# Layer normalisation moved from VectorE to ScalarE in a two-layer attention, Mamba and expert kernel

## The chip, the cores and the metric

The kernel runs on one core of one Trainium2 chip. The metric is the device time of one execution in microseconds (us); three runs are given by their median. The engines are TensorE (PE in the profile, its weight loads PEld), VectorE (DVE), ScalarE (ACT), GpSimd (POOL) and SyncE (SP), which only issues transfers here.

## The reference

```python
x = L0_attn_x                      # [8, 512, 128]: 8 batches of 512 tokens, float32
xn = _layernorm(x)                 # (x - mean) / sqrt(var + 1e-5), over the 128 features
s = attention(xn)                  # q, k, v; no token attends to itself; softmax
g = _silu(experts(xn))             # 8 experts of 256, two per token, gated
x = x + s * g
xn = _layernorm(x)
s = mamba(xn)                      # rmsnorm, in_proj, conv of 4 taps, selective scan
                                   # (256 channels x 16 states), out_proj, + xn
g = _silu(switch_experts(xn))      # 8 experts of 512, one per token, with a norm of its own
x = x + s * g
```

## The kernel before

The 8 batches are handled one after the other; 512 tokens lie as 4 tiles of 128 tokens (one token per partition, 128 features along the row), and after a transpose as one tile of 128 features by 512 tokens. All arithmetic of the matrix products is float32.

The work of a batch is cut into groups of steps: A is the first layer (layer norm `ln0` and `xn`, transpose `xT`, gate logits `gl` and `gate`, `q`, `k`, `v`, scores `s`, transposes `p` of the weights, output `o`, expert products `h` and `m`, and `silu`, which adds the result to x and signals `x1`). H is the head of the second layer (`ln1`, `xm`, transposes `hT` and `x1T`, `xi` and `z` with the convolution, `u`, `bc`, `dl`, `ln`, `du`, and the routing `sc`, `rk`, `put`). S is the scan: 32 steps, each with a decay `d` on ACT, a product with B and a scan on DVE (lines 1296 and 1303), a product with C on POOL (`p`, line 1470), and sums over states on PE (`a`, line 888) or POOL (`e`, line 1477); `b` spreads a row of B over the partitions on PE (line 877), `c` loads a row of C. F is the second expert layer on tokens sorted by expert (`xs`, `h`, `y`, `get`, `ft`, `silu`), and C the end of a batch (`y`, `op`, `out`).

Every engine works through one list that is written before the kernel starts. A table `ROWS` gives for each step its place in an iteration, counted in iterations of 32 scan slots, then offsets in slots for ACT, DVE and POOL, and the PSUM bank that it uses. Group A runs two batches ahead of the scan, H one ahead, C one behind, so one iteration holds A of batch b+2, H of b+1, S and F of b and C of b-1. A second table, `OWN`, has places of their own for A and H of batch 0 and A of batch 1, which make up the prologue. An engine is strictly in order: a step that waits holds up all that stands behind it on its engine. PE and SP follow the places alone.

The two layer norms are made in three parts. DVE takes mean and variance of each token (`moments`, lines 1118 and 1121). POOL computes `rstd` = (var + eps) to the power -0.5, and for the second norm also `rstd2`, the scale of the rmsnorm that follows it. DVE then writes `(x - mean) * rstd` tile by tile, as `xn` (line 1146) into `xn_tok` and as `xm` (line 1214) into `xn1_tok`. In the step `xm` ACT scales `xn1_tok` by `rstd2` into `ht_tok` (line 1001), from which PE makes `hT`. In the trace `qkv` stands for the tensor that holds `xn_tok`, `xn_tok` for the one written by `xm`, and `hx` for `ht_tok` and `hT`. Almost all of ACT's work is recorded under line 944.

## Time and profile before

| | |
|---|---|
| median of 3 runs | 982.8 us (982.41 to 982.96) |
| the profiled execution | 983.75 us |
| its span, first to last instruction | 981.9 us |
| PE busy | 855.8 us, 87% |
| DVE busy | 810.0 us, 82% |
| ACT busy | 608.9 us, 62% |
| POOL busy | 587.6 us, 60% |
| mean granted TensorE clock | 0.936 of full speed |

The profile is of one execution. Busy time is the time in which an engine runs an instruction; the chain that ended last is followed backwards from the last instruction, at each step to what released it or to what stood before it on its engine. A group of instructions is named by line, engine, operation and tiles (output <- inputs), and the idle time in front of it by what ended it.

### The profile page before, as it was taken

To read this page: it belongs to the slowest core of one execution; us is meant where nothing else is said; L and a number is where in the kernel's file an instruction comes from. 1 tells how busy PE (TensorE), PEld (TensorE's weight loads), DVE (VectorE), ACT (ScalarE), POOL (GpSimd) and SP (SyncE) were. 2 spreads that over 40 slices of the span, in tenths; PEclk is the share of its full clock that TensorE was granted. 3 is DMA by queue.
4 is the path that set the end of the run, shared out by engine and by line. 5 is a ranking of instruction groups with operands and counts; after the bars stand their busy time and mean duration, and the time that the engine had idled before them with its cause. 6 is when DMAs were issued, how large, how long until landed. Compare 5 with 4: busy or idle time off the path is not lost.

```text
span 981.9 us, 15767 instructions
## 1 busy us (share of the span) xinstructions
PE 855.8 (87%) x4624; PEld 582.9 (59%) x4624; DVE 810.0 (82%) x1542; ACT 608.9 (62%) x1315; POOL 587.6 (60%) x524
## 2 busy tenths in 40 slices
PE   5997897999699978999799969999799977684995
PEld 3773475766467745766477736776477645452762
DVE  4244537999989889999999998998999989886995
ACT  3424644868467766778477765778477765574661
POOL 0010202848856695848766694848765697669665
PEclk9977699999899999999999998999999989796998
DMA  7200103224323334324323243225322234324542
GB/s 263 88 0 1 44 12 105 72 80 97 115 65 90 96 94 128 76 76 121 94 89 93 75 115 99 76 78 131 100 85 79 77 101 138 98 72 113 156 132 51
DMA packets 79428, 90.27 MB, mean 92 GB/s; under 512 B 8450, under 2 KB 49906, under 8 KB 78834
## 3 DMA queue, kind: packets, MB, share of 16 engines
q1 hardware_dynamic: 77298, 85.07, 29.5%
q0 software_dynamic: 2048, 4.20, 1.5%
q8 instruction: 40, 0.66, 0.3%
q14 instruction: 42, 0.34, 0.1%
HBM read 52.96 MB, written 13.04 MB: 67 GB/s over the span
## 4 chain that ended last, share of the span: by engine, by line
PE 55%; DVE 21%; issue 9%; POOL 8%; ACT 5%; SPq 1%; DMA 1%; DVEq 0%; POOLq 0%
PE work L823 10%; PE work L829 9%; DVE st L1303 7%; PE work L854 5%; PE yacc L888 5%; PE work L864 5%; PE work L752 3%; POOL st L1470 3%; PE work L773 3%; DVE b_row L1296 2%; PE work L796 2%; PE work L743 2%; PE b_row L877 2%; ACT prob L944 1%; PE work L725 1%
## 5 line engine op out<-in xcount | busy, mean ns | idle before, releaser
L1470 POOL TENSOR_TENSOR st<-st,Cs 128x512 f32<-128x512 f32 x249 | 316.8, 1278 | 178.1 <-DVE st L1303 162.9
L944 ACT ACTIVATE dA<-delta,Aneg 128x512 f32<-128x512 f32 x256 | 175.5, 723 | 20.6 <-POOL du L1431 10.7
L888 PE MATMUL yacc<-st,w_ident 128*128 128x512 f32 x256 | 143.6, 650 | 19.5 <-POOL st L1470 19.1
L1303 DVE TENSOR_TENSOR_SCAN st<-dA,dbu 128x512 f32<-128x512 f32 x128 | 154.7, 1209 | 1.4 <-PE yacc L888 0.6
L1303 DVE TENSOR_TENSOR_SCAN st<-dA,b_row 128x512 f32<-128x512 f32 x123 | 148.7, 1209 | 3.1 <-POOL y L1477 3.1
L829 PEld LDWEIGHTS work<-w_w2a,hid 128*128 128x128 f32 x1024 | 124.3, 195 | 29.4 <-issue 13.0
L944 ACT ACTIVATE hsT<-work,hs 128x128 f32<-128x128 f32 x352 | 99.7, 370 | 61.0 <-PE work L854 60.3
L823 PE MATMUL work<-xnT,w_w1a 128*128 128x512 f32 x256 | 134.5, 615 | 0.7 <-ACT dt L944 0.7
L1477 POOL TENSOR_TENSOR y<-y,st 128x512 f32<-128x512 f32 x105 | 133.2, 1269 | 3.0
L829 PE MATMUL work<-w_w2a,hid 128*128 128x128 f32 x1024 | 127.3, 279 | 5.2 <-ACT hid L944 5.2
L944 ACT ACTIVATE hid<-work,w_b1a 128x512 f32<-128x512 f32 x128 | 87.9, 688 | 66.5 <-PE work L823 62.1
L1188 DVE SCALAR_TENSOR_TENSOR acc<-work,gates,acc 128x128 f32<-128x128 f32 x256 | 71.0, 339 | 50.0 <-PE work L829 46.2
L854 PEld LDWEIGHTS work<-xsT,hs 128*128 128x128 f32 x704 | 92.6, 202 | 20.8 <-issue 12.3
L854 PE MATMUL work<-xsT,hs 128*128 128x128 f32 x704 | 98.2, 287 | 1.2 <-ACT hsT L944 1.2
L864 PE MATMUL work<-w_w2f,hsT 128*128 x704 | 98.8, 284 | 0.0
L864 PEld LDWEIGHTS work<-w_w2f,hsT 128*128 128x128 f32 x704 | 86.4, 193 | 20.0 <-issue 17.8
L1296 DVE TENSOR_TENSOR dbu<-b_row,du 128x512 f32<-128x512 f32 x123 | 85.4, 695 | 14.8 <-PE b_row L877 7.3
L1296 DVE TENSOR_TENSOR b_row<-b_row,du 128x512 f32<-128x512 f32 x123 | 84.0, 683 | 2.7
L877 PE MATMUL b_row<-bc,sel_b 96*128 96x512 bf16 x123 | 48.8, 400 | 35.5 <-DVE st L1303 35.5
L888 PEld LDWEIGHTS yacc<-st,w_ident 128*128 128x128 f32 x256 | 46.0, 204 | 56.3 <-POOL st L1470 28.6
L1418 POOL TENSOR_TENSOR ve<-mv,eps 128x4 f32<-128x4 f32 x16 | 3.2, 201 | 113.9 <-DVE mv L1121 113.9
L1440 POOL DMA_INDIRECT xs_dram<-xn_tok,pos x32 | 32.5, 1016 | 51.9 <-DVE pos L1271 43.7
(187 smaller groups left out, 1315.0 us busy)
## 6 DMA issues: line engine op xcount, KB each, us to landing
Cs<-c_dram SPq DMA_DIRECT2D x128, 256.0 KB
hs<-w_w1f SPq DMA_DIRECT2D x88, 258.0 KB, 2.4
xs_in<-xs_dram SPq DMA_DIRECT2D x16, 256.0 KB
ys_dram<-ys SPq DMA_DIRECT2D x16, 256.0 KB, 2.2
w_w1f<-in_w1f_dram SPq DMA_DIRECT2D x1, 2064.0 KB, 7.7
x_in<-in_x_dram SPq DMA_DIRECT2D x8, 256.0 KB
w_w2f<-in_w2f_dram SPq DMA_DIRECT2D x1, 2048.0 KB, 12.8
kept_dram<-x_tok SPq DMA_DIRECT2D x8, 256.0 KB, 2.4
```

The costliest lines, as they stand in the source:

```text
L823: last = mm(w[:], W["w1a"][:, i * 128:(i + 1) * 128], xnT[:], start=True, stop=True)
L829: last = mm(w[:, t * 128:(t + 1) * 128], hid[:, c % 4, t * 128:(t + 1) * 128], W["w2a"][:, c * 128:(c + 1) * 128], start=(c == PER * i), s ...
L854: last = mm(w[:, c * 128:(c + 1) * 128], w1s[:, i % 2, c * 128:(c + 1) * 128], xsT[:, i // 4 % 2, i % 4 * 128:(i % 4 + 1) * 128], start=Tr ...
L864: last = mm(r, hsT[:, i % 2, c * 128:(c + 1) * 128], W["w2f"][:, bass.ds(e * H1 + c * 128, 128)], start=False, stop=(c == HC - 1))
L877: mm(rows_bank(n, b)[:], row_of(n), bc3[:, par], start=True, stop=True).then_inc(sig["B_in"], 1)
L888: mm(yacc[:], ident[:], state(s), start=False, stop=(n == NS - 1)).then_inc(sig["y_sum0"], 1)
L944: return nc.scalar.activation(out, in_, func, **k)
L1188: last = V.scalar_tensor_tensor(acc[:, t], w[:, t * 128:(t + 1) * 128], gates[:, t, i:i + 1], acc[:, t], ALU.mult, ALU.add)
L1296: V.tensor_tensor((dbu0, rows_bank(n, b))[h][:], rows_bank(n, b)[:], du[:, par, h], ALU.mult).then_inc(sig["dBu"], 1)
L1303: V.tensor_tensor_scan(state(s), dA[:, s % DECAYS], (dbu0, rows_bank(n, b))[h][:], 0.0, ALU.mult, ALU.add).then_inc(sig["scan"], 1)
L1470: G.tensor_tensor(state(s), state(s), Cs[:, b.of(NS, n) % C_BUFS], ALU.mult).then_inc(sig["P"], 1)
L1477: G.tensor_tensor(y1[:], y1[:], state(s), ALU.add).then_inc(sig["y_sum1"], 1)
```

## The change

The last part of both norms moves from DVE to ACT. ACT computes `x * rstd + shift` per token, as one activation with a scale and a shift per partition, and POOL makes `shift` = 0 - mean * rstd by two more operations on 128x4 elements, linked to the one before by waits. ACT's step `xn` is new in its list; its step `xm` now makes `xn1_tok` first and then, as before, `ht_tok`. Two waits come with it: ACT's `xm` waits for `opx` of two batches before, the last reader of the half of `xn1_tok` that it overwrites; DVE's write of `x_tok` waits for `xn1` of the batch before. All places, offsets and prologue places are new. The order of the groups and their distance in batches stay. The lines of `ROWS` that the prediction speaks of:

```diff
...
-    ("F", "xs", 0, 0.01820, 1, 5, 7, 0),
...
-    ("A", "xT", 0, 0.05523, 0, 2, 0, 1),
...
-    ("A", "ln0", 0, 0.03157, -1, -1, -1, None),
-    ("A", "xn", 0, 0.06785, 0, -2, -2, None),
...
-    ("A", "gl", 0, 0.08355, 1, 1, 6, 0),
...
-    ("A", "q", 0, 0.09246, 1, 7, -1, 3),
...
-    ("A", "k", 0, 0.08641, -1, 7, 2, 2),
...
-    ("H", "ln1", 0, 0.30272, -3, -2, -1, None),
-    ("H", "xm", 0, 0.24559, 5, 3, -4, None),
...
-    ("H", "cw", 0, 0.69621, -4, 1, 3, None),
...
-    ("A", "m", 6, 0.88321, 8, 0, 4, 1),
...
-    ("S", "c", 15, 0.87337, -1, 6, 3, None),
-    ("A", "m", 7, 0.91105, 8, 1, 3, 3),
...
-    ("H", "keep", 0, 0.86292, -1, 7, -3, None),
-    ("H", "fetch", 0, 0.99456, 3, 7, 2, None),
...
+    ("F", "xs", 0, 0.00177, 1, 7, 1, 3),
...
+    ("A", "xT", 0, 0.06669, -1, -1, 3, 3),
...
+    ("A", "ln0", 0, 0.03416, -1, -1, -1, None),
+    ("A", "xn", 0, 0.04999, 0, -1, -4, None),
...
+    ("A", "gl", 0, 0.07446, -1, 0, 8, 0),
...
+    ("A", "q", 0, 0.12685, -2, 7, -3, 3),
...
+    ("A", "k", 0, 0.10789, -1, 7, 0, 3),
...
+    ("H", "ln1", 0, 0.28984, -4, -3, -4, None),
+    ("H", "xm", 0, 0.29673, 1, 3, -4, None),
...
+    ("H", "cw", 0, 0.99045, -2, 4, 0, None),
...
+    ("A", "m", 6, 0.95524, 7, 0, 1, 1),
...
+    ("S", "c", 15, 1.00111, 4, 7, 2, None),
+    ("A", "m", 7, 0.96005, 5, 1, 5, 2),
...
+    ("H", "keep", 0, 0.57657, 1, 7, -3, None),
+    ("H", "fetch", 0, 0.78823, 0, 7, 2, None),
...
```

The code:

```diff
@@ -494,6 +494,8 @@
         rstd1 = sb("rstd1", [128, NT])
         q2 = sb("q2", [128, NT])
         rstd2 = sb("rstd2", [128, NT])
+        shift, shift1 = sb("shift", [128, NT]), sb("shift1", [128, NT])
+        zeros = sb("zeros", [128, NT])
         xn1_tok = sb("xn1_tok", [128, 2, NT, D])
         xn1T = sb("xn1T", [128, T])
         u = sb("u", [128, 2, NH, T])
@@ -995,7 +997,17 @@
                 elif name == "hT":
                     filled(act, g, step, b)
                     go(hT, w[:], ACT.Copy).then_inc(fr, 1)
+                elif name == "xn":
+                    act.wait_ge(sig["rstd0"], b.of(1, 1))
+                    for t in range(NT):
+                        last = go(xn_tok[:, t], x_in[:, par, t], ACT.Identity, scale=rstd[:, t:t + 1], bias=shift[:, t:t + 1])
+                    last.then_inc(sig["xn0"], 1)
                 elif name == "xm":
+                    act.wait_ge(sig["rstd1"], b.of(1, 1))
+                    since(act, sig["opx"], b.of(1, -1))
+                    for t in range(NT):
+                        last = go(xn1_tok[:, par, t], x_tok[:, t], ACT.Identity, scale=rstd1[:, t:t + 1], bias=shift1[:, t:t + 1])
+                    last.then_inc(sig["xn1"], 1)
                     act.wait_ge(sig["xn1"], b.of(1, 1))
                     for t in range(NT):
                         last = go(ht_tok[:, t], xn1_tok[:, par, t], ACT.Copy, scale=rstd2[:, t:t + 1])
@@ -1140,12 +1152,6 @@
                 if name == "ln0":
                     dve.wait_ge(sig["x_in%d" % par], 16 * (b.n // 2 + 1))
                     moments(g, x_in[:, par], stats, mv, "mean0")
-                elif name == "xn":
-                    dve.wait_ge(sig["rstd0"], b.of(1, 1))
-                    for t in range(NT):
-                        last = V.tensor_scalar(xn_tok[:, t], x_in[:, par, t], mv[:, t, 0:1], rstd[:, t:t + 1],
-                                               ALU.subtract, ALU.mult)
-                    last.then_inc(sig["xn0"], 1)
                 elif name == "v":
                     filled(dve, g, step, b)
                     V.tensor_tensor(v_tok, tiles(w[:]), W["bv"][:].unsqueeze(1).broadcast_to([128, NT, D]), ALU.add
@@ -1202,18 +1208,13 @@
                     emptied(dve, g, ("o", NT - 1), b)
                     lk(g, V.tensor_tensor(r, r, s_tok, ALU.mult))
                     since(dve, sig["kept"], b.of(16))
+                    since(dve, sig["xn1"], b.of(1))
                     V.tensor_tensor(x_tok[:], x_in[:, par], r, ALU.add).then_inc(sig["x1"], 1)
                     dve.wait_ge(sig["x1"], b.of(1, 1))
                     dve.sem_inc(free_of(g, ("m", E - 1), b), 1)
                 elif name == "ln1":
                     dve.wait_ge(sig["x1"], b.of(1, 1))
                     moments(g, x_tok, stats1, mv1, "mean1")
-                elif name == "xm":
-                    dve.wait_ge(sig["rstd1"], b.of(1, 1))
-                    for t in range(NT):
-                        last = V.tensor_scalar(xn1_tok[:, par, t], x_tok[:, t], mv1[:, t, 0:1], rstd1[:, t:t + 1],
-                                               ALU.subtract, ALU.mult)
-                    last.then_inc(sig["xn1"], 1)
                 elif name == "xi":
                     dve.wait_ge(sig["cv_a"], b.of(NH, i + 1))
                     cw = W["conv_w"]
@@ -1395,6 +1396,7 @@
 
             V.memset(neghalf[:], -0.5)
             V.memset(eps[:], EPS)
+            V.memset(zeros[:], 0.0)
             V.memset(fe[:], 0.0)
             V.memset(ones_b[:], 1.0)
             V.memset(ones8[:], 1.0)
@@ -1416,7 +1418,9 @@
                     mv_k, ve_k, rstd_k = (mv, ve, rstd) if k == "0" else (mv1, ve1, rstd1)
                     pool.wait_ge(sig["mean" + k], b.of(1, 1))
                     lk(g, G.tensor_tensor(ve_k[:], mv_k[:, :, 1], eps[:], ALU.add))
-                    last = G.tensor_tensor(rstd_k[:], ve_k[:], neghalf[:], ALU.pow)
+                    lk(g, G.tensor_tensor(rstd_k[:], ve_k[:], neghalf[:], ALU.pow))
+                    lk(g, G.tensor_tensor(ve_k[:], mv_k[:, :, 0], rstd_k[:], ALU.mult))
+                    last = G.tensor_tensor((shift if k == "0" else shift1)[:], zeros[:], ve_k[:], ALU.subtract)
                     if name == "ln0":
                         last.then_inc(sig["rstd0"], 1)
                     else:
```

## Rows read from the trace of the kernel before

**Rows 1.** The page: busy time of each engine, and the chain that ended last.

```profile
PE 855.8 (87%) x4624; PEld 582.9 (59%) x4624; DVE 810.0 (82%) x1542; ACT 608.9 (62%) x1315; POOL 587.6 (60%) x524
...
PE 55%; DVE 21%; issue 9%; POOL 8%; ACT 5%; SPq 1%; DMA 1%; DVEq 0%; POOLq 0%
```

**Rows 2.** Windows: busy us of each engine in each stretch.

```profile
core 0: us, PE busy (x) PEld busy (x) DVE busy (x) ACT busy (x) POOL busy (x), PEclk, DMA share, GB/s
...
382.37:491.08 108.71, 100.01 (x569) 69.24 (x568) 100.14 (x190) 75.46 (x165) 75.93 (x68) 0.97 0.33 95
...
394.00:460.00 66.00, 65.76 (x402) 47.30 (x401) 61.62 (x112) 50.07 (x113) 46.53 (x43) 1.00 0.29 81
460.00:491.00 31.00, 22.55 (x96) 13.95 (x96) 28.13 (x51) 17.49 (x34) 25.34 (x23) 0.89 0.43 118
```

**Rows 3.** The chain that ended last, by line, of 460 to 491 us.

```profile
by line: DVE st L1303 22.1%; issue 15.3%; DVE acc L1188 6.7%; PE work L725 5.9%; DVE b_row L1296 4.8%; DVE qkv L1146 4.6%; DVE work L1276 4.6%; DVE work L1275 4.2%; DVE dbu L1296 4.2%; ACT L944 4.1%; DVE stats L1118 2.8%; PE work L722 2.6%;
```

**Rows 4.** Waits of 460 to 491 us: us in total, times, longest.

```profile
PE b_row L877 <- DVE st L1303: 4.9, 3, 2.4
...
PE work L847 <- ACT xsT L944: 1.6, 1, 1.6
...
PE yacc L886 <- DVE du L1317: 1.0, 1, 1.0
...
PE work L829 <- ACT hid L944: 0.9, 1, 0.9
```

**Rows 5.** Groups of the two normalisations on DVE, whole run.

```profile
L1214 DVE TENSOR_SCALAR xn_tok<-x_tok,mv,rstd 128x128 f32<-128x128 f32 x32 | 29.8, 992 | 3.3 <-POOL rstd L1428 3.3
...
L1146 DVE TENSOR_SCALAR qkv<-x_in,mv,rstd 128x128 f32<-128x128 f32 x32 | 11.4, 417 | 4.3 <-POOL rstd L1419 4.3
```

**Rows 6.** Timeline: `xm` on DVE beside POOL, and in the prologue.

```profile
406.10 4.12 DVE L1214 TENSOR_SCALAR xn_tok<-x_tok,mv,rstd 128x128 f32<-128x128 f32 x4
...
406.26 2.53 POOL L1470 TENSOR_TENSOR st<-st,Cs 128x512 f32<-128x512 f32 x2
...
66.17 1.11 DVE L1214 TENSOR_SCALAR xn_tok<-x_tok,mv,rstd 128x128 f32<-128x128 f32 x4 [3.33 <-POOL rstd L1428]
```

**Rows 7.** ACT's activations by group; a run of four; two pieces of the chain.

```profile
L944 ACT ACTIVATE hid<-work,w_b1a 128x512 f32<-128x512 f32 x128 | 87.9, 688 | 66.5 <-PE work L823 62.1 <-issue 2.1 <-PE work L829 2.0
...
L944 ACT ACTIVATE cv<-work,w_conv_b,w_conv_w 128x512 f32<-128x512 f32 x16 | 12.6, 788 | 7.7 <-PE work L773 7.7
...
410.26 1.28 ACT L944 ACTIVATE hx<-xn_tok,rstd 128x128 f32<-128x128 f32 x4 [0.61 <-DVE xn_tok L1214]
...
406.27 1.79 PE work L829 x16
...
414.08 1.79 PE work L829 x16
```

**Rows 8.** Timeline: POOL's small linked operations.

```profile
401.86 0.20 POOL L1425 TENSOR_TENSOR q<-rstd 128x4 f32<-128x4 f32 x1
...
402.14 0.20 POOL L1426 TENSOR_TENSOR q<-q,mv 128x4 f32<-128x4 f32 x1
```

**Rows 9.** Timeline: around `xn` in the followed iteration.

```profile
483.11 2.17 ACT L944 ACTIVATE hsT<-work,hs 128x128 f32<-128x128 f32 x8 [0.30 <-PE work L854]
483.15 1.05 POOL L1419 TENSOR_TENSOR rstd<-ve,neghalf 128x4 f32<-128x4 f32 x1
...
484.88 1.42 DVE L1146 TENSOR_SCALAR qkv<-x_in,mv,rstd 128x128 f32<-128x128 f32 x4
...
487.47 0.60 ACT L944 ACTIVATE xnT<-work 128x512 f32<-128x512 f32 x1 [2.20 <-PE work L718]
```

**Rows 10.** Timeline: the first boundary, and the last layer norm.

```profile
157.26 2.06 DVE L1146 TENSOR_SCALAR qkv<-x_in,mv,rstd 128x128 f32<-128x128 f32 x4 [1.44 <-POOL rstd L1419]
...
830.20 1.01 POOL L1428 TENSOR_TENSOR rstd<-q,neghalf 128x4 f32<-128x4 f32 x1
...
837.86 1.09 PE L765 MATMUL work<-w_ident,hx 128*128 128x128 f32 x4 [3.51 <-ACT hx L944]
```

More of the change, by code:

```diff
@@ L325 @@
     ("A", 0): (
[4 rows of a table removed]
[4 rows of a table added]
     ),
     ("H", 0): (
-        -1.11900, -1.08467, -1.01476, -0.83547, -0.90068, -0.85797, -0.89443, -0.84069, -0.83471, -0.83140, -0.82978, -0.62226,
-        -0.81859, -0.79895, -0.81765, -0.90515, -0.81371, -0.74442, -0.61163, -0.90703, -0.69090, -0.71827, -0.58703, -0.54773,
-        -0.50916, -0.42023, -1.08490, -1.30874,
+        -1.11411, -1.06978, -1.05742, -0.89565, -0.90279, -0.83828, -0.88733, -0.81603, -0.81528, -0.80089, -0.79422, -0.57863,
+        -0.79157, -0.74780, -0.77419, -0.79303, -0.73709, -0.72833, -0.62595, -0.89555, -0.69538, -0.77574, -0.66455, -0.53536,
+        -0.45046, -0.49154, -0.77058, -0.61446,
     ),
     ("A", 1): (
[4 rows of a table removed]
[4 rows of a table added]
     ),
```

510 rows, old and new, of tables (OWN, ROWS) are left out of this document.

## The prediction, made before the changed kernel was run

> **What bounds the kernel now.** I read the page's head and chain first [rows 1]. The reader is to see that PE and DVE are busy 87% and 82% of the span, ACT and POOL 62% and 60%, and that the chain of work that ended last runs over PE for 55% and over DVE for 21%, over ACT for 5%. So two engines share the end between them, and work taken off DVE can count, but not all of it.
>
> Next the windows, by stage [rows 2]. From 164 to 819 us the kernel repeats one pattern: six iterations, of which one is 382.37 to 491.08, 108.7 us long. In it PE is busy 100.0 us, DVE 100.1, ACT 75.5, POOL 75.9. Cut in two, PE is full from 394 to 460 (65.76 of 66 us) and has holes from 460 to 491 (22.55 of 31 us, at a mean granted clock of 0.89), while DVE is busy 28.13 of these 31. The chain in the second part says it again [rows 3]: DVE's scan alone is 22.1%, and the DVE normalisation L1146 4.6%, that is 1.42 us. The waits in it [rows 4] name what PE lacks there: 4.9 us in which `b_row` waits for a scan, 1.0 us for L1317.
>
> So the iteration is PE's for some 66 us and mostly DVE's for some 31 us. But DVE is 93% busy in the first part too (61.62 of 66): it carries its backlog into the second.
>
> **The change, part by part.** *Off DVE.* Per batch four `xm` and four `xn` instructions. All 64 are 29.8 + 11.4 = 41.2 us of DVE's 810, 992 ns for one of `xm` (L1214) and 417 for one of `xn` (L1146) [rows 5]. In the iteration that I follow the four take 4.12 us, while POOL runs two 128x512 products back to back in 2.53 us; at 66 us, where POOL has nothing of that kind, four take 1.11 us [rows 6]. So the price on DVE is 4.12 us for `xm` and 1.42 us for `xn` [rows 6, 9]: 5.5 us of DVE's 100.1 per iteration. The Trainium skill's page "SBUF — State Buffer", section "Who interferes with whom", says why: some VectorE instructions and GpSimd's share a port pair, and the one that comes second waits out the whole instruction of the other, while ScalarE waits on neither. By it four `xm` would cost up to four POOL products, 5.1 us; the trace is near that with 4.12. With 5.1 the term of `xm` in the sum below would be 1.8 instead of 1.5.
>
> *Onto ACT.* Four activations with one per-partition operand take 1.28 us in a run; an operand more costs 0.10 us on 512 columns (788 against 688 ns) [rows 7]. Four with scale and shift are then 1.4 to 1.7 us; I take 1.6, since the added 0.1 can fall in each of the four. ACT gets 3.2 us more per iteration: 75.5 becomes 78.7 of 108.7. For `xm` the row scaling (`ht`) follows in the same step, so 1.6 + 1.3 = 2.9 us stand in front of what is next on ACT: the evacuation of `h3` and two decays. Expert product `m1`, the first to need `h3`, starts 8 us after `m0` (406.1 and 414.1 [rows 7]), and the decays run up to four ahead of the scans, so I cost this at nothing; if that cover is gone, it is 1.6 us per iteration. `xn` stands between the evacuations of F's `h0` and `h1`, where ACT now is idle 2.2 us, waiting for `xT` [rows 9].
>
> *Onto POOL.* Two linked operations on 128x4 more per layer norm, 0.20 us and 0.07 to 0.08 us of gap each, as the rows of `q2` show [rows 8]: 0.54 us per norm, 1.1 us per iteration, on the way from the moments to the signal. POOL is 75.9 of 108.7 us busy. The memset of `zeros` stands among its like at the start, while PE waits for the weights: nothing.
>
> *Waits added.* ACT waits for `opx` of two batches before (`xm`), and DVE's x1 for `xn1` of the batch before; both are one iteration old when they are asked, so they cost nothing. DVE no longer waits for `rstd0` and `rstd1`, with its scans queued behind.
>
> *Places.* PE's order at the boundary becomes `xT`, `y0`, `gl`, `op`, `k`, `q` (before: `xT`, `gl`, `k`, `q`, `op`), `m6` and `m7` come some two scan slots later, and F's first transpose gets bank 3 where the second has bank 0, so that the second no longer waits for ACT to empty the first (1.6 us of PE per iteration [rows 4]). PE then still waits 1.0 us for L1317, so I count this at nothing (bounds 0 and 1.6). On SP's queue `keep`, `cw`, `c15` and `fetch` move. The first three wait for signals older than their places. `fetch` now waits for the four `put` transfers ahead of `c13` and `c14`; POOL issues the puts in one run before state product `p21`, and `c13` serves `p26`, so this is nothing too, unless the puts are late, when POOL's products would wait. Nothing else in the tables removes work. The new order as such I put at nothing; what it can move is PE's idle time, 8.7 us of an iteration, and a third of that either way would be 3 us per iteration, 17 in all, which the cases A and C span.
>
> **The sum.** In the second part of the iteration `xn` leaves DVE [rows 9]: 1.42 off, 0.54 of POOL on, 0.9 us gained. For PE nothing is gained by it: `rstd0` comes at 484.2 + 0.5 = 484.7, `xn` ends at 486.3 as it does now, the evacuation of `h1` behind it at 487.4, and that of `xT` starts then, now at 487.5. The bounds for this term are 0 and 1.42. `xm` leaves DVE where PE is full, so it pays only through backlog: between 0 and 4.12 us. Half of it is 2.1, DVE's share of the chain (21%) times it 0.9; I take the middle, 1.5. Together 2.4 us per iteration, times six 14.4.
>
> Outside of the pattern [rows 10]: the first boundary (157 us) has DVE idle 1.44 us for `rstd0` and then 2.06 us in `xn`, 3.5 in all, of which DVE's scans can win up to 3.0; half, 1.5. In the last layer norm PE waits 3.51 us for `ht`, until 837.9; new, `rstd1` comes at 831.2 + 0.5, and 1.6 + 1.3 us on ACT with some 0.2 of hand-over end near 834.8: up to 3.0, of which I take 2.0, since scans bound the tail too. In the prologue the way to `hT` is one chain [rows 6]: 1.11 us becomes 1.6, and 0.54 comes on POOL's side, for which DVE waits 3.33 us there already: 1.0 us lost. The other prologue places only reorder what PE does when full, or when the Mamba chain is alone: nothing, within 3 us.
>
> Sum: 14.4 + 1.5 + 2.0 - 1.0 = 16.9 us. The profiled execution has 983.75 us, its span 981.9 and 1.85 around it; it becomes 966.9. The median of the runs is 0.95 us below the profiled time, so the prediction is 966 us.
>
> **The rivals.**
> *A, the whole release counts.* DVE is the bound all along: its 100.1 busy us and 8.6 us of hand-over per iteration move together. For it: 28.13 of 31 us busy in the second part. Against it: PE has no hole for 66 us [rows 2]. 5.0 us per iteration (5.5 less 0.54) are 30, with 5 outside (both upper bounds less the prologue's 1.0) 35: 948 us. Chance 0.14.
> *B, only a little counts.* PE binds, `xm` gives back nothing, `xn` 0.9 us: 5.4 + 2.5 outside, 975 us. For it: `xm` lies where PE is full. Against it: what PE lacks later is scans, and `xm` delays these. The Trainium skill's page "ScalarE: Activation LUTs", "Rules for kernel authors", wants additions and products on VectorE since it is the faster; by it the exchange is a loss of speed, which holds here for undisturbed instructions (1.11 against 1.28 us), not for `xm` as it runs. Chance 0.22.
> *C, ACT takes the place of DVE.* The 2.9 us block of `xm` and the 1.6 of `xn` delay `hid`, decays and `xnT` in ACT's queue. PE already waits for `hid` 0.9 us per iteration. If DVE's release is worth the 0.9 of B and all 3.2 us come on the chain, an iteration is 2.3 us longer: 14, with 1 lost outside 998 us; from half of the 3.2 it costs 0.7 each, 988 us. It decides if more than 0.9 us (B) to 2.4 us (mine) of the 3.2 lie on the chain. Against it: ACT is idle 33 us of each iteration. Chance 0.13.
> *D, nothing to be measured*: gains and the new order cancel, 983 us. Chance 0.06.
>
> **How the numbers follow.** Mine, 958 to 972 us, has 0.45. Faster is mine, A and B: 0.81. Same 0.06 (0.2%, 2 us, is about what a measurement of this kernel can tell), slower 0.13. For 8 in 10 the range runs from 954 (half of A left out) to 984 us (B and D whole, C left out).
>
> **What would show it.** DVE busy 41 us less (769), ACT 22 to 26 more (some 633), POOL 8 to 10 more plus nothing for its products. An iteration of 106.3 us. DVE's share of the chain below 21%, PE's above 55%. `b_row` waiting for scans less than 4.9 us per iteration. The normalisations on ACT near 480 ns each. Wrong: ACT above 10% of the chain, `hid` waits grown beyond 1 us per iteration (C), an iteration at 108 (B) or 104 (A), or DVE's scan inputs slower than 0.69 us because they now meet POOL more often.

## The result, and the profile after

The changed kernel takes 978.09 us in the median of 20 runs (974.61 to 984.63), the kernel before beside it on the same chip 981.47 us (20 runs, 979.82 to 983.40): a ratio of 0.9967, 95% interval 0.9951 to 0.9983, or 3.4 us faster. Forecast were 16.9. The changed kernel's runs spread over 10 us, those of before over 3.6. The profiled execution has 977.57 us and a span of 975.8, 6.1 below the span of before; against the medians' 3.4 some 2.7 us of these 6.1 are the choice of executions.

The page's head and chain, to be laid beside [rows 1]:

```profile
PE 854.6 (88%) x4624; PEld 583.0 (60%) x4624; DVE 777.3 (80%) x1479; ACT 632.0 (65%) x1379; POOL 592.7 (61%) x556
...
PE 53%; POOL 17%; DVE 15%; issue 10%; ACT 4%; SPq 1%; DMA 0%; DVEq 0%; POOLq 0%
```

The work went where it should: DVE is 32.7 us less busy, ACT 23.1 more, POOL 5.1 more. What the reader is to see is in the chain: DVE fell from 21% to 15%, but POOL rose from 8% to 17%.

Windows of the changed kernel: one iteration, and another one cut into its first and its end part, as [rows 2] has them for before:

```profile
378.00:487.25 109.25, 100.11 (x568) 69.57 (x568) 95.65 (x181) 78.29 (x172) 76.51 (x71) 0.97 0.30 94
500.00:565.00 65.00, 64.71 (x399) 46.88 (x399) 57.12 (x108) 51.06 (x114) 45.88 (x44) 1.00 0.30 94
565.00:596.30 31.30, 22.99 (x105) 15.04 (x104) 27.19 (x47) 18.93 (x38) 26.87 (x26) 0.89 0.36 117
```

The columns behind the length are busy us of PE, PE's weight loads, DVE, ACT and POOL, then the granted clock, the DMA share and GB/s. DVE is busy 95.65 us of an iteration instead of 100.14, and the iteration is no shorter. In the first part PE is full as before, and DVE is busy 57.12 of 65 us instead of 61.62 of 66: what it lost in work it has as idle time. In the end part little moves: PE 22.99 us (22.55 before), DVE 27.19 (28.13), though `xn`'s 1.42 us are gone from it.

To compare stretches I mark each iteration by one event, the second of the four activations L944 (after: L946) that write `prob`:

| | starts of the mark in iterations 1 to 6, us | mean of the five iterations between | from the last mark to the end |
|---|---|---|---|
| before | 173.24, 283.39, 392.12, 500.83, 611.04, 719.77 | 109.31 | 262.1 |
| after | 171.83, 279.58, 388.50, 497.76, 606.81, 716.15 | 108.86 | 259.7 |

Up to the first mark 1.4 us are gained (forecast: 0.5, the first boundary's 1.5 less the prologue's 1.0). Of the five iterations the first is shorter by 2.4 and the fourth by 1.2, the other three are longer by 0.2 to 0.6; the four behind the first together take 436.57 us against 436.38. Forecast were 12.0 for the five. From the last mark on 2.5 are gained (forecast 4.4, the sixth iteration and the last layer norm).

### The profile page after: what moved, and what is told of

It reads as the page before. It is cut to its first block, busy times and chain, and to the rows that moved or that the text cites. A ratio compares the mean times of both kernels' runs of the same rounds, so it can differ in the third digit from the quotient of the medians.

```text
span 975.8 us, 15806 instructions
## 1 busy us (share of the span) xinstructions
PE 854.6 (88%) x4624; PEld 583.0 (60%) x4624; DVE 777.3 (80%) x1479; ACT 632.0 (65%) x1379; POOL 592.7 (61%) x556
## 4 chain that ended last, share of the span: by engine, by line
PE 53%; POOL 17%; DVE 15%; issue 10%; ACT 4%; SPq 1%; DMA 0%; DVEq 0%; POOLq 0%
PE work L825 9%; PE work L831 7%; POOL st L1474 7%; PE work L856 7%; DVE st L1304 6%; PE work L866 5%; PE yacc L890 5%; POOL y L1481 4%; PE work L754 3%; PE work L775 3%; POOL fe L1461 3%; POOL du L1435 2%; PE work L745 2%; PE work L798 2%; ACT prob L946 1%
## 5 line engine op out<-in xcount | busy, mean ns | idle before, releaser
L946 ACT ACTIVATE dA<-delta,Aneg 128x512 f32<-128x512 f32 x256 | 176.0, 722 | 9.6 <-DVE st L1304 9.1
L890 PE MATMUL yacc<-st,w_ident 128*128 128x512 f32 x256 | 141.3, 637 | 27.2 <-POOL st L1474 27.2
L831 PEld LDWEIGHTS work<-w_w2a,hid 128*128 128x128 f32 x1024 | 121.5, 192 | 27.6 <-issue 13.0
L825 PE MATMUL work<-xnT,w_w1a 128*128 128x512 f32 x256 | 130.4, 600 | 5.9 <-ACT ys L946 3.8
L946 ACT ACTIVATE hsT<-work,hs 128x128 f32<-128x128 f32 x352 | 100.6, 373 | 49.5 <-PE work L856 49.5
L831 PE MATMUL work<-w_w2a,hid 128*128 128x128 f32 x1024 | 124.9, 276 | 7.6 <-DVE delta L1278 7.6
L856 PE MATMUL work<-xsT,hs 128*128 128x128 f32 x704 | 106.6, 303 | 19.1 <-ACT xsT L946 17.9
L856 PEld LDWEIGHTS work<-xsT,hs 128*128 128x128 f32 x704 | 100.8, 216 | 37.0 <-ACT xsT L946 19.4
L946 ACT ACTIVATE hid<-work,w_b1a 128x512 f32<-128x512 f32 x128 | 86.8, 684 | 51.8 <-PE work L825 34.0
L1297 DVE TENSOR_TENSOR dbu<-b_row,du 128x512 f32<-128x512 f32 x123 | 85.5, 695 | 30.6 <-PE b_row L879 21.3
L866 PE MATMUL work<-w_w2f,hsT 128*128 x704 | 100.6, 287 | 0.0
L866 PEld LDWEIGHTS work<-w_w2f,hsT 128*128 128x128 f32 x704 | 87.7, 196 | 13.9 <-issue 10.7
L890 PEld LDWEIGHTS yacc<-st,w_ident 128*128 128x128 f32 x256 | 47.2, 203 | 72.7 <-POOL st L1474 42.4
L1444 POOL DMA_INDIRECT xs_dram<-xn_tok,pos x32 | 31.9, 998 | 52.4 <-DVE pos L1272 45.2
```

The lines of the kernel that those rows point to most:

```text
L825: last = mm(w[:], W["w1a"][:, i * 128:(i + 1) * 128], xnT[:], start=True, stop=True)
L831: last = mm(w[:, t * 128:(t + 1) * 128], hid[:, c % 4, t * 128:(t + 1) * 128], W["w2a"][:, c * 128:(c + 1) * 128], start=(c == PER * i), s ...
L856: last = mm(w[:, c * 128:(c + 1) * 128], w1s[:, i % 2, c * 128:(c + 1) * 128], xsT[:, i // 4 % 2, i % 4 * 128:(i % 4 + 1) * 128], start=Tr ...
L866: last = mm(r, hsT[:, i % 2, c * 128:(c + 1) * 128], W["w2f"][:, bass.ds(e * H1 + c * 128, 128)], start=False, stop=(c == HC - 1))
L890: mm(yacc[:], ident[:], state(s), start=False, stop=(n == NS - 1)).then_inc(sig["y_sum0"], 1)
L946: return nc.scalar.activation(out, in_, func, **k)
```

## Why 4.5 us off DVE did not show: the end part of an iteration

The timeline of POOL in the end part of the changed kernel, with the first instruction that the result releases on ACT and on PE (the bracket is the idle time ahead of an instruction):

```profile
552.59 1.09 POOL L1444 DMA_INDIRECT xs_dram<-xn_tok,pos  x1 [2.55 <-DVE pos L1272]
...
557.50 3.73 POOL L1474 TENSOR_TENSOR st<-st,Cs 128x512 f32<-128x512 f32 x3
561.18 1.26 POOL L1481 TENSOR_TENSOR y<-y,st 128x512 f32<-128x512 f32 x1
...
570.08 1.01 POOL L1461 DMA_INDIRECT fe<-ys_dram,pos  x1
...
576.03 1.29 POOL L1435 TENSOR_TENSOR du<-delta,u 128x512 f32<-128x512 f32 x1
...
583.38 1.26 POOL L1481 TENSOR_TENSOR y<-y,st 128x512 f32<-128x512 f32 x1
584.61 1.25 POOL L1453 TENSOR_TENSOR fe<-fe,xn_tok 128x512 f32<-128x512 f32 x1
...
585.90 0.63 ACT L946 ACTIVATE ys<-fe 128x512 f32<-128x512 f32 x1 [1.89 <-POOL fe L1453]
586.43 1.07 ACT L946 ACTIVATE xsT<-work 128x512 f32<-128x512 f32 x2
...
587.11 3.75 PE L856 MATMUL work<-xsT,hs 128*128 128x128 f32 x16 [2.84 <-ACT xsT L946]
```

`pos` on DVE, which comes at a fixed point of PE's full part (POOL's first put starts 55.0 us after the mark in all five iterations before, 54.8 after), releases the four puts (L1444). From there to the end of `ft` (L1453, at 585.86) POOL never waits for another engine, for 33.3 us; the gaps in it are of 0.3 us at most. In the kernel before the same run is as long:

```profile
447.13 1.08 POOL L1440 DMA_INDIRECT xs_dram<-xn_tok,pos  x1 [2.77 <-DVE pos L1271]
...
479.06 1.26 POOL L1449 TENSOR_TENSOR fe<-fe,xn_tok 128x512 f32<-128x512 f32 x1
...
482.01 2.01 PE L854 MATMUL work<-xsT,hs 128*128 128x128 f32 x16
```

447.13 to 480.32 is 33.2 us. Behind `ft` ACT's `silu` (the row `ys<-fe`) and `xsT` stand in order, and PE waits for them, 2.84 us here. PE's waits of 565 to 596.3 us (in total, times, longest) are to be laid beside [rows 4]:

```profile
PE work L856 <- ACT xsT L946: 2.8, 1, 2.8
...
PE yacc L890 <- POOL st L1474: 2.3, 2, 1.5
...
PE b_row L879 <- DVE st L1304: 1.1, 1, 1.1
```

The wait for a scan fell from 4.9 to 1.1 us, as forecast, and waits for POOL and for what stands behind it came in its place. The chain of the same stretch says it in shares:

```profile
by line: POOL st L1474 19.3%; issue 15.2%; POOL y L1481 13.6%; PE work L856 12.0%; POOL fe L1461 10.5%; POOL du L1435 8.2%; PE yacc L888 5.5%; PE yacc L890 4.0%; POOL fe L1453 3.9%; PE work L866 3.0%; PE work L724 2.6%; ACT ys L946 2.0%; AC
...
584.64 1.23 POOL fe L1453
...
585.90 0.63 ACT ys L946
586.53 0.49 ACT xsT L946
...
587.11 3.75 PE work L856 x16
```

In the same stretch of before the chain ran over DVE's scans [rows 3].

The rows hold a second reason, TensorE's clock. The sixteen products behind `xsT` take 2.01 us before (L854, granted clock 1.00) and 3.75 us after (L856, granted clock 0.50, the lower of its two levels, 1.2 GHz; it fell at 586.4, while PE stood waiting for `xsT`). Both kernels spend 6.8 us of an iteration at the lower level, the changed one 3.4 in its first. What differs is where it falls. Before, it meets these products in two iterations of five (3.62 us; from the end of `ft` to the next mark are then 22.0 us instead of 20.5). After, it meets them in all five: in four they take 3.75 us and that stretch 20.8 to 21.0, in the first 2.88 us and 19.6. At the same clock level on these products the stretch behind `ft` is thus some 1.2 us shorter than before, and 0.9 of that lies ahead of them: PE starts them 1.25 us after `ft` instead of 2.11. In the three iterations that had 20.5 us before, the place of the slow stretch takes this gain back, and a little more. No run isolates the clock; this is read from the rows of one execution of each kernel.

My theory for the rest (the joint bound): two engines, POOL and DVE, reach the end of this part within about a microsecond of each other, both before and after, and whoever is relieved alone only waits for the other. The rivals: POOL alone is the bound, so DVE's work does not matter; DVE's work counts as predicted, and the new places or ACT take the gain away again; or only the change made POOL the bound.

## Experiments

Ratios are to the kernel before, run on the same chip, with their 95% intervals.

### Less work on POOL, on DVE, and on both, in both kernels

Two cuts, which leave a part of y, of `delta` and of the expert sums uncomputed, made in the changed kernel and in the kernel before. On POOL (`y_sum1` for states 10 to 15 on a quarter of the columns):

```diff
-                    G.tensor_tensor(y1[:], y1[:], state(s), ALU.add).then_inc(sig["y_sum1"], 1)
+                    c = 128 if n >= 10 else T
+                    G.tensor_tensor(y1[:, 0:c], y1[:, 0:c], state(s)[:, 0:c], ALU.add).then_inc(sig["y_sum1"], 1)
```

On DVE (two of the three operations that make `delta`, and the sums of the last two experts):

```diff
+                    c = 128
-                    lk(g, V.scalar_tensor_tensor(r[:], r[:], 1.0, ab[:, i], ALU.subtract, ALU.subtract))
-                    lk(g, V.tensor_tensor(r[:], rl[:, i], r[:], ALU.subtract))
+                    lk(g, V.scalar_tensor_tensor(r[:, 0:c], r[:, 0:c], 1.0, ab[:, i, 0:c], ALU.subtract, ALU.subtract))
+                    lk(g, V.tensor_tensor(r[:, 0:c], rl[:, i, 0:c], r[:, 0:c], ALU.subtract))
...
-                    for t in range(NT):
+                    for t in range(NT if i < 6 else 1):
...
```

The changed kernel, less on POOL. 

> The changed kernel in which POOL's last six additions into y of each batch but the last (step e, n of 10 to 15) handle 128 of 512 columns: part of y is left out. Takes some 5 us of POOL out of the run from pos to F's add, and nothing from DVE. Theory P (POOL's run closes the iteration): iteration down from 109.1 by 3 to 5 us, 945 to 962 us. Theory D (DVE's scans close it, POOL only looks full because it follows them): below 1 us per iteration, 972 to 980 us.

The changed kernel, less on DVE. 

> The changed kernel in which DVE does less in the same part of the iteration: two of the three operations behind delta (lines with r) handle 128 of 512 columns, and the additions of the last two experts handle one tile of four; that part of the result is left out. 3.7 us off DVE, nothing off POOL. P: no gain, below 1 us per iteration, 972 to 980 us. D: 2 to 3.7 us per iteration, 954 to 966 us.

The changed kernel, both. 

> The changed kernel with both cuts at once: the additions of y for states 10 to 15 on 128 of 512 columns (some 5 us per iteration off POOL, which gave 1.3 us alone) and two of the operations that make delta on 128 columns and the last two experts' sums on one tile of four (3.7 us off DVE in the end part, which gave 0.3 to 0.6 alone). It leaves out that part of the work. Joint bound (the end part of an iteration is closed by POOL and, a little over 1 us behind it, by DVE): together they give clearly more than the 1.6 to 1.9 us of their sum, 3 us or more per iteration, so 105.5 to 106 us per iteration and 955 to 962 us. POOL alone is the bound and PE's products come next: no more than with the POOL cut alone, 971 us. Two independent small gains: their sum, 967 us.

The kernel before, less on DVE. 

> The kernel before with the same 3.7 us per iteration taken off DVE in the end part, nothing added elsewhere and all places left. It leaves out the same part of the work. My prediction's reading (DVE is 28 of 31 us busy there, so it bounds the end part): 2 to 3 us per iteration, 965 to 970 us. Joint bound (POOL runs without a hole for 33 us there and closes the part whatever DVE does): at most 0.6 us per iteration, 978 to 982 us. This is the test of the step in which I took work off DVE to shorten the end part.

The kernel before, less on POOL. 

> The kernel before, its own places, with the additions of y for states 10 to 15 on 128 of 512 columns (in the changed kernel the same cut took 33 us off POOL and 1.3 us off an iteration). It leaves out that part of y. Joint bound (the end part of an iteration is closed by POOL first and DVE close behind, in the kernel before as in the changed one): 1 to 2 us per iteration, 970 to 976 us. DVE is the bound in the kernel before and POOL only in the changed one: less than 0.3 us per iteration, 979 to 983 us.

The kernel before, both. 

> The kernel before with that cut on POOL and the one on DVE together (two of the operations of delta on 128 columns, the last two experts' sums on one tile of four; alone on this kernel: 984 us, no gain). Joint bound: clearly more than the two cuts alone, 3 us or more per iteration, 955 to 963 us; DVE's part would then be worth 8 us or more here where it was worth nothing alone. POOL alone is the bound and PE next: what the POOL cut gives alone. DVE's cut hurts in itself (its changed order of arrival): above the POOL cut alone.

Measured:

| | median us | ratio | mean iteration, us | from the last mark, us |
|---|---|---|---|---|
| before, beside each | 981.1 to 982.0 | 1 | 109.31 | 262.1 |
| before, less POOL | 973.15 | 0.9891 (0.9853 to 0.9930) | 108.54 | 257.6 |
| before, less DVE | 983.98 | 1.0027 (1.0007 to 1.0046) | 109.37 | 263.9 |
| before, both | 964.30 | 0.9812 (0.9781 to 0.9842) | 106.80 | 256.9 |
| after | 978.09 | 0.9967 (0.9951 to 0.9983) | 108.86 | 259.7 |
| after, less POOL | 970.85 | 0.9902 (0.9864 to 0.9940) | 107.53 | 258.8 |
| after, less DVE | 974.68 | 0.9923 (0.9897 to 0.9950) | 108.54 | 262.5 |
| after, both | 954.95 | 0.9738 (0.9714 to 0.9762) | 105.35 | 253.7 |

The last two columns are of one execution each. The profile of the changed kernel with less on DVE is of its slowest run (979.51 us), so its two columns stand too high; that of the kernel before with less on DVE is of its fastest of five (979.74 us), so its columns stand too low. The cuts took 32 to 34 us off POOL's busy time and 18 (before) or 24 us (after) off DVE's, by the heads of the pages; I had put DVE's at 3.7 us per batch, it is 2.2 and 3.0. In the kernel before, DVE's cut alone gives nothing, POOL's alone 1.09%; together they give 1.88%, so DVE's is worth 0.8% once POOL is relieved. In the changed kernel, taken against its 0.9967, they give 0.65% and 0.44% alone and 2.30% together, twice their sum; the single gains are known to some 0.4% and 0.3% only, the sum of both upper ends is still below 2.30%. So all single-engine readings fall: POOL alone (DVE's cut would add nothing to POOL's), and DVE as I had predicted it (its cut would pay by itself in the kernel before). The joint bound's own ranges were met for the kernel before with less on POOL and all but met for the changed kernel with both cuts; the kernel before came out 2.0 us above its range with less on DVE and 1.3 above with both. POOL's cut in the changed kernel (970.85) fits neither of the two theories stated for it. The same iterations cut at POOL's run, five of each kernel:

| us | mark to first put | first put to end of `ft` | end of `ft` to next mark |
|---|---|---|---|
| before | 55.0 | 33.2 | 20.5 to 22.0 |
| before, less POOL | 55.0 | 31.5 to 32.9 | 20.9 to 23.0 |
| before, less DVE | 55.0 to 55.4 | 33.2 | 20.9 to 21.3 |
| before, both | 55.0 to 55.4 | 30.5 to 31.0 | 20.6 to 22.0 |
| after | 54.8 | 33.3 to 33.7 | 19.6 to 21.0 |
| after, less POOL | 54.8 | 31.0 to 31.4 | 20.9 to 22.3 |
| after, less DVE | 54.8 | 33.3 | 19.6 to 21.0 |
| after, both | 54.8 | 31.0 to 31.4 | 19.2 to 19.9 |

No relief of DVE alone, neither the change nor the cut, moves the middle column; POOL's cut does. And where POOL alone is relieved in the changed kernel, the last column grows, until DVE's cut brings it down (20.9 and 19.2 us, both in iterations at the full clock). In the kernel before the clock is not what makes the pair worth more than its parts: at a granted clock of 0.97 an iteration of the kernel before takes 109.3 us in the mean, with less on POOL 109.1 (one iteration), with less on DVE 109.3 to 109.4, with both 106.9 to 107.7. But of the 0.8 us of POOL's cut alone most goes with a clock of 0.98, which three of its five iterations had. In the changed kernel the clock's part in the 2.30% is open: with both cuts three of five iterations ran at the full clock, with DVE's alone none. Chains of the kernel before with less on DVE, and of the changed kernel with less on POOL:

```profile
PE 50%; POOL 19%; DVE 14%; issue 11%; ACT 5%; SPq 1%; DMA 0%; DVEq 0%; POOLq 0%
```

```profile
PE 54%; DVE 27%; issue 10%; ACT 4%; POOL 4%; SPq 1%; DVEq 0%; DMA 0%; POOLq 0%; ACTq 0%
```

Less on DVE moves the chain to POOL (8% to 19%), less on POOL moves it to DVE (15% to 27%). The first of these two shows in the kernel before what the change itself did: it takes DVE down in the chain and POOL up. And POOL's cut in the kernel before (0.8 us per iteration, a little below the 1 to 2 expected; the rest of its gain lies in the tail, 4.5 us) shows, with the middle column above, that POOL held the way to `ft` already then; the change did not make it the bound.

### The move without the new places

Table of before, arithmetic of after. Only `xn`'s place had to go, to just ahead of `xT`:

```diff
-    ("A", "xn", 0, 0.06785, 0, -2, -2, None),
+    ("A", "xn", 0, 0.04370, 0, -2, -2, None),
```

> The two norms on ACT with the shift on POOL, under the old places (only ACT's xn step is set just ahead of its transpose, between the evacuations of F's h0 and h1). Theory P (POOL's run from the positions `pos` to F's add, 33.2 us in both profiles without a hole, closes each iteration, so DVE time is not what it lacks): no gain in the iteration, 978 to 984 us, iteration 108.7 to 109.3 us. Theory A (ACT's in-order queue ate what DVE gave back): slower than the changed kernel, 982 to 990. Theory O (the new places cost what the move brought): 966 to 974, iteration near 107.

Measured 988.27 us, ratio 1.0063 (1.0048 to 1.0077): the move by itself is a loss. The prologue is 3.5 us longer and the iterations 110.2 us on average, 0.8 longer. DVE is 37.9 us less busy and nothing comes of it. At the boundary that I had counted `xn`'s 0.9 us on:

```profile
378.75 0.69 DVE L1318 TENSOR_TENSOR du<-yacc,zg 128x512 f32<-128x512 f32 x1
...
379.27 1.65 ACT L946 ACTIVATE qkv<-x_in,shift,rstd 128x128 f32<-128x128 f32 x4 [0.51 <-POOL shift L1423]
...
379.49 1.12 PE L888 MATMUL yacc<-u,diagD 128*128 128x512 f32 x2 [0.96 <-DVE du L1318]
...
380.51 1.12 PE L890 MATMUL yacc<-st,w_ident 128*128 128x512 f32 x2
...
381.48 0.60 PE L720 MATMUL work<-w_ident,qkv 128*128 128x128 f32 x4
```

`xn` is ready at 380.9, but PE has its own products (L888, L890) between the old batch's last result and `xT` (L720), up to 381.5. At this boundary an `xn` that is shorter or elsewhere is hidden by them. Why the move alone loses is not settled. Of the 0.8 us per iteration 0.5 lie between the mark and the first put (55.5 us instead of 55.0), the rest behind the end of `ft` (21.4 us in the mean instead of 21.1). ACT has 9% of this run's chain (5% before), and 988 us lies in the range named for ACT's queue (theory A), so in the old places that rival (C of the prediction) stands.

### The new places without the move

Table of after, arithmetic of before; first as it is, then with the offset of `xm` on DVE, which is empty in the changed kernel, set as early as before:

```diff
-    ("H", "xm", 0, 0.29673, 1, 3, -4, None),
+    ("H", "xm", 0, 0.29673, 1, 1, -4, None),
```

> The new places with the norms on DVE as before. P: the places bring what little was gained (prologue, first iteration, tail), 976 to 984 us. O: places are the harm, above 986 us. A: no ACT load, so faster than the changed kernel, 970 to 976.

> The new places with the norms on DVE as before, and with xm on DVE two slots earlier than the unused offset in the new table had put it, as early as in the kernel before. If the new order brought the gain and the move only made room: 974 to 986 us. If the new order works only with the norms on ACT: above 990.

Measured 1043.3 us, ratio 1.0627 (1.0607 to 1.0647), and 1019.97 us, ratio 1.0398 (1.0376 to 1.0421), iterations of 115.0 us. The first is no clean test, since ACT waits 65.2 us in all for `xm`; in the second it is still 43.3 us. What stands: the new places are far worse than the old ones for the old division of work. They are not a gain that comes on top.

### One norm alone back on DVE, in the new places

```diff
-    ("H", "xm", 0, 0.29673, 1, 3, -4, None),
+    ("H", "xm", 0, 0.29673, 3, 1, -4, None),
...
+                        last = V.tensor_scalar(xn1_tok[:, par, t], x_tok[:, t], mv1[:, t, 0:1], rstd1[:, t:t + 1],
```

> The changed kernel with xm alone back on VectorE (its step on DVE at offset 1, ACT's at 3, two slots behind, so that ACT does not wait for it). If xm's release is worth nothing because PE is full there and DVE's gain only becomes waiting: 978 to 981 us, the pattern at 109 us. If xm on DVE is the part for which the new places have no room (with both norms on DVE they took 114 to 117 us per iteration): above 1000 us. By my prediction's term it would cost 1.5 us per iteration, 987 us.

> The changed kernel with xn alone back on VectorE at its own place and offset -1. If xn's release is worth nothing (PE's own products stand between, or POOL closes the end part anyway): 978 to 981 us. By my prediction's term: 0.9 to 1.4 us per iteration, 984 to 986 us. If xn is the part for which the new places have no room, because with ACT's evacuations moved before it DVE's scans wait for rstd0 behind a POOL that runs without a hole: above 1000 us.

Measured with `xm` back 991.18 us, ratio 1.0105 (1.0087 to 1.0123), with `xn` back 994.40 us, ratio 1.0130 (1.0109 to 1.0152); neither came out as any of my theories had it. Against the changed kernel these are 13.1 and 16.3 us. `xm` costs 0.7 us per iteration in the mean, and 9.5 us behind the last mark; ACT waits for it 32.6 us in all (15.1 in the kernel before), so a part of this may be my offset. Between the mark and the first put it costs 1.4 us (56.25 instead of 54.83 in the iterations behind the first), about my term of 1.5; the mean hides half of that, since four of its five iterations have a granted clock of 0.98 and only one of the changed kernel's has. `xn` costs 3.8 us per iteration (112.65, at a granted clock of 0.95), nearly all of it behind the end of `ft` (24.0 to 24.8 us instead of 19.6 to 21.0), and its rows say where:

```profile
489.60 0.20 POOL L1424 TENSOR_TENSOR shift<-zeros,ve 128x4 f32<-128x4 f32 x1
489.83 2.04 DVE L1153 TENSOR_SCALAR qkv<-x_in,mv,rstd 128x128 f32<-128x128 f32 x4 [2.00 <-POOL shift L1424]
...
493.37 0.69 DVE L1319 TENSOR_TENSOR du<-yacc,zg 128x512 f32<-128x512 f32 x1
...
494.11 1.12 PE L888 MATMUL yacc<-u,diagD 128*128 128x512 f32 x2 [2.41 <-DVE du L1319]
```

In the new places `ln0` follows `ft` and one addition into y on POOL without a gap, so on DVE `xn` waits 2.00 us for it and runs 2.04 us, and the end of the old batch (L1319), on which PE waits 2.41 us, stands behind. With `xn` on ACT these 4 us go beside. So the wait that I counted at nothing ("DVE no longer waits for `rstd0` ..., with its scans queued behind") is worth most in these places, and little in the old ones, where DVE is idle ahead of `xn` for 4.3 us in the whole run and 1.4 at most at once.

### Real relief for POOL: the product `du` on DVE

These two leave nothing out. The two products `du` per batch (1.27 us each on POOL) are made by DVE right after `delta`, in the changed kernel and in the kernel before:

```diff
+                    V.tensor_tensor(du[:, par, i], delta[:, par, i], u[:, par, i], ALU.mult).then_inc(sig["du%d" % i], 1)
...
-                    G.tensor_tensor(du[:, par, i], delta[:, par, i], u[:, par, i], ALU.mult).then_inc(sig["du%d" % i], 1)
```

> The changed kernel with the two products delta*u (step du) computed by DVE (0.69 us each) instead of POOL (1.27 each), all else equal. P: POOL's run gets 2.5 us shorter in each iteration and DVE has 5 us to spare, so the iteration falls by 1.5 to 2.5 us: 962 to 971 us. A or O (POOL has slack, DVE gets 1.4 us more): 978 to 986.

> The same two products on DVE in the kernel before, where DVE still has the norms. P: POOL's run is shorter by 2.5 us but DVE, 28.1 of 31 us busy in that part, gets 1.4 more there: 974 to 982 us, less gain than in the changed kernel. If DVE alone was the bound before: 986 to 994.

Measured 995.44 us, ratio 1.0146 (1.0118 to 1.0175), and 987.38 us, ratio 1.0057 (1.0039 to 1.0075). POOL and DVE in the changed kernel:

```profile
697.51 3.16 DVE L1280 TENSOR_TENSOR du<-delta,u 128x512 f32<-128x512 f32 x1
...
697.61 2.51 POOL L1473 TENSOR_TENSOR st<-st,Cs 128x512 f32<-128x512 f32 x2
```

and the group of the product over the whole run:

```profile
L1280 DVE TENSOR_TENSOR du<-delta,u 128x512 f32<-128x512 f32 x16 | 27.3, 1706 | 0.5
```

The product takes 1.7 us on DVE in the mean and 3.16 where it meets two products of POOL; so POOL's 2.5 us per batch became 3.4 us on DVE. POOL's run to `ft` got no shorter by it: in the kernel before it is 33.5 to 33.6 us with a wait of 2.4 us for a scan in it, in the changed kernel 35.0 to 35.4 with 3.6 us or more of waits for scans. This is the joint bound with all the work computed: what POOL was spared it waits for DVE. Both ranges, 962 to 971 and 974 to 982 us, were missed. The third version keeps one input in PSUM: `delta` is finished in its bank, DVE multiplies from there, and ACT copies `delta` out (its step `du` at offset 3 instead of -1).

```diff
+                    V.tensor_tensor(du[:, par, i], r[:], u[:, par, i], ALU.mult).then_inc(sig["du%d" % i], 1)
...
+                elif name == "du":
+                    act.wait_ge(sig["du%d" % i], b.of(1, 1))
+                    go(delta[:, par, i], bank(g, ("dl", i), b)[:], ACT.Copy).then_inc(free_of(g, ("dl", i), b), 1)
```

> The changed kernel with step du on DVE, this time with one input in PSUM: delta is finished in PSUM, DVE multiplies it by u there, ACT copies it to SBUF. DVE 1.4 us more, ACT 1.2 more, POOL 2.5 less per iteration. In the run with both inputs in SBUF one such product took 3.16 us beside two POOL products; here it should take 0.69. P: 1 to 2.5 us per iteration less, 962 to 972 us. D: 0.5 to 1.5 us more, 980 to 988 us.

Measured 994.24 us, ratio 1.0132 (1.0109 to 1.0155). The product is now fast, but the bank is free later, because ACT's copy stands behind its wait for the gets. The group, and the waits of one end part:

```profile
L1282 DVE TENSOR_TENSOR du<-work,u 128x512 f32<-128x512 f32 x16 | 11.1, 691 | 0.5
...
PE work L831 <- ACT delta L946: 3.0, 1, 3.0
...
PE work L825 <- ACT delta L946: 1.6, 1, 1.6
```

PE's 4.6 us in this end part are more than the 2.5 us that POOL was relieved of. The first stretch did get shorter (32.5 to 32.9 us from the first put to the end of `ft`), the one behind longer (22.5 to 24.4 us). No experiment that computes everything beats the changed kernel; the two cuts only show what lies behind the bound.

## Why the prediction was wrong, step by step

**The failed step** is "So the iteration is PE's for some 66 us and mostly DVE's for some 31 us", and with it both terms of the pattern, 0.9 us for `xn` and 1.5 for the backlog of `xm`, 14.4 of the 16.9 us. I had judged POOL by its average, "75.9 of 108.7 us busy", where its timeline has no hole for 33 us and ends with `ft`, on which ACT and then PE wait. Measured: 2.2 us for the five iterations between the marks instead of 12.0, and nothing in the last four taken together. The cut on the kernel before is the direct test: 2.2 us per batch off DVE gave no gain (ratio 1.0027). The second thing that the sum left out is the clock: the prediction names the mean of 0.89 in the end part and prices nothing by it, and the place of the slow stretch took back the 1.2 us gained behind `ft` in three of five iterations. Of these 1.2 us 0.9 lie where the term for F's first transpose, "I count this at nothing (bounds 0 and 1.6)", had them.

**The backlog of `xm`.** "It carries its backlog into the second": it does not show in the time. The four instructions left DVE in PE's full part, and DVE's busy time there fell by 3.5 us per 65 us, but that of the end part by 0.9 only, less than `xn`'s 1.42. What DVE gained it spent waiting for PE: its scan inputs waited for `b_row` 7.3 us in the whole run before, 21.3 after:

```profile
DVE dbu L1297 <- PE b_row L879: 21.3, 8, 3.0
```

**The term of `xn`.** In the old places PE's own products cover it (the move alone); in the new ones it is worth 3.8 us per iteration, but only against an order that DVE's `xn` fits badly.

**The places.** "The new order as such I put at nothing": this was wrong in kind. The move alone is 1.0063, the new places with the old division 1.04 or more, both together 0.9967. Neither part is a term of its own with a fixed size, so a sum of parts could not come out. Against the move alone the new places are worth 10 us; of the 12.8 us between the two profiled spans 4.9 lie up to the first mark, 6.5 in the five iterations and 1.5 behind. What in the order of PE gives the rest I did not take apart, and it stays open. The spread of 10 us goes with the granted clock: the seven fastest runs of the changed kernel (974.6 to 975.7 us) have 0.944 to 0.947, the six slowest (980.8 to 984.6) 0.936 to 0.941; which causes which, and why the changed kernel has runs of both kinds, is open.

**The costs on the engines** were right for ACT, 632.0 us (633 forecast). POOL has 5.1 more (8 to 10). DVE has 777 us (769 forecast): of the 8 us that are missing 6.8 are one small scan per batch, `endt` of 128x8 (L1261), which takes 1.4 us in the eight before and 8.2 after, because its new place falls beside a product of POOL. ACT's normalisations take 492 and 520 ns by group, near the 480 named, and four in a run 1.65 us (1.6). ACT is at 4% of the chain (5% before) and PE waits 1.6 us for `hid` in the whole run (5.2 before); rival C did not happen in the new places, nor did `fetch` or the added waits cost anything that a view shows. ACT's block of four normalisations and four scalings:

```profile
511.87 1.68 ACT L946 ACTIVATE xn_tok<-x_tok,shift,rstd 128x128 f32<-128x128 f32 x4
513.58 1.28 ACT L946 ACTIVATE hx<-xn_tok,rstd 128x128 f32<-128x128 f32 x4
514.77 0.67 ACT L946 ACTIVATE hid<-work,w_b1a 128x512 f32<-128x512 f32 x1
```

**Outside of the pattern.** Up to the first mark 1.4 us instead of 0.5, from the last on 2.5 instead of 4.4. In the tail, PE's product behind the last norm (L767, at 833.88) no longer waits for ACT, where it waited 3.51 us [rows 10]; it now stands behind PE's own L866. The Mamba chain of the prologue lost as forecast: 7.62 us of ACT's idle time end with POOL's `rstd`, then come 1.65 us.

**Of the rivals** B came nearest, 975 us, with the reason that `xm` gives nothing back; but its `xn` term was as wrong as mine, so that it came near is luck. My chance of 0.81 for faster holds by its sign alone.

## What to carry to other kernels

An engine at 70% of an iteration (POOL, 76.51 of 109.25 us here) can be the bound of its end part: read each engine's timeline back from the event that releases the next stage, and look for the last idle time ahead of it, before any average is used. Where two engines reach that event within a microsecond or so, price a relief of one as the gap between them and not as its size; a cut of each alone and of both (here 0.65%, 0.44% and 2.30%) finds such a pair. Look at the granted clock of the products on the way before the time of a stretch is put down to who waits for whom. And with a written-out order of work, a change of the engine and a change of the order are worth something only together.

## What the runs showed of the hardware

A DVE product of two tensors in SBUF takes 3.16 us beside two products of POOL (697.51 above, and much the same in six of the sixteen), where the same with one input in PSUM takes 0.69 us throughout (16 of them in 11.1 us) although POOL is as busy. The Trainium skill, page "SBUF — State Buffer", section "Who interferes with whom", says this: a VectorE instruction with two SBUF inputs contends with a GpSimd one that reads SBUF, one with at most one SBUF input, outside the 2-port modes, does not, and the later one is blocked whole. The trace agrees in size: 3.16 us is about 0.69 plus the 2.51 us of POOL's two products. It shows more than one instruction waited out, and in its record the blocked product starts 0.1 us ahead of the first of the two, so it does not bear out the order. The same price fell on the small scan `endt`: 0.17 us alone, 1.15 to 1.18 beside a POOL product in six of its eight. So such work moved from POOL to DVE costs more than either engine's price, and the same product from PSUM pays its own.
